# Seat scatter, lookup and edge-row gathers of a graph network, from loops with index copies to written-out DMAs

## The reference

```python
h = jnp.maximum(_layernorm(x, axis=-1), 0.0)
# layer 0, twice: norm = dinv[s] * dinv[d], with every node also its own neighbour
agg = jax.ops.segment_sum(norm[:, None] * h[s], d, num_segments=n); h = agg @ W.T + b
# layer 1
agg = jax.ops.segment_sum(jax.nn.relu(h[src] + edge_attr), dst, num_segments=n)
# layer 2, 8 steps: softmax of the edges of one destination, then
h = jax.ops.segment_sum(h[src] * a[:, None], dst, num_segments=n); th = th + h * temp[k + 1]
# layer 3, 10 steps: src_norm from the count of each source, dst_norm from that of each destination
h = jax.ops.segment_sum((h * src_norm[:, None])[src], dst, num_segments=n) * dst_norm[:, None]
out = out + w[step + 1] * h
```

## Time and profile before

| | |
|---|---|
| three timed runs | 8374.17, 8385.81, 8390.06 us; median 8385.81 |
| the profiled execution | 8379.78 us, its span 8378.1 us |
| POOL busy | 5656.5 us (68%), 5478 instructions |
| DVE busy | 5415.4 us (65%), 18625 instructions |
| PE busy | 1686.8 us (20%) |
| ACT busy | 822.6 us (10%) |
| chain that ended last, by engine | POOL 46%, issue 22%, DVE 20%, DMA 7% |
| of it, POOL gathers into `pair` | 5% |
| of it, POOL scatters into `seatmap` | 5% |

### The profile page before, as it was taken

One profiled execution on the slowest core, in us unless ns is written; L12 is line 12 of the kernel. 1 busy time (PEld: TensorE's weight loads), 2 busy tenths in 40 slices (PEclk: granted clock), 3 DMA queues, 4 the chain that ended last, 5 costly groups with the idle time before them and its releaser, 6 DMA issues.

```text
span 8378.1 us, 61926 instructions
## 1 busy us (share of the span) xinstructions
PE 1686.8 (20%) x7784; PEld 1230.3 (15%) x7784; DVE 5415.4 (65%) x18625; ACT 822.6 (10%) x2010; POOL 5656.5 (68%) x5478
## 2 busy tenths in 40 slices
PE   5744435310355135500022102000000000000000
PEld 1233324210244023400022101000000000000000
DVE  6778868758988634367788788666556664445520
ACT  0011112100122431100000000000006000000000
POOL 6777767656777767667677573666650767777767
PEclk8755555555555555555555555555555555555555
DMA  7034424310355433933444213243232222433310
GB/s 260 0 88 96 95 63 108 74 34 6 88 126 131 102 96 99 299 85 106 122 110 111 68 46 81 48 44 46 40 33 87 47 61 50 42 43 43 38 22 19
DMA packets 1198007, 661.31 MB, mean 79 GB/s; under 512 B 1057323, under 2 KB 1070560, under 8 KB 1195204
## 3 DMA queue, kind: packets, MB, share of 16 engines
q10 hardware_dynamic: 880608, 373.78, 16.4%
q0 software_dynamic: 174720, 155.54, 12.7%
q1 hardware_dynamic: 142436, 129.95, 5.2%
HBM read 236.69 MB, written 425.58 MB: 79 GB/s over the span
## 4 chain that ended last, share of the span: by engine, by line
POOL 46%; issue 22%; DVE 20%; DMA 7%; ACT 3%; DVEq 1%; POOLq 1%; ACTq 1%; SPq 0%; PE 0%
POOL G L575 20%; POOL X L575 12%; DVE G L2154 5%; POOL pair L575 5%; POOL seatmap L579 5%; POOL out L579 4%; ACT wide_block L1160 2%; POOL wide_block L575 1%; DVE xm L1648 1%; DVE st L1618 1%; DVE G L2466 1%; DMA raw<-G 1%; DMA G<-alt_d,idxC 1%; DMA G<-tab,idxA 1%; ACT rowsB L1160 1%
## 5 line engine op out<-in xcount | busy, mean ns | idle before, releaser
L575 POOL DMA_INDIRECT G<-tab,idxA x1008 | 1082.4, 1074 | 341.1 <-issue 322.1
L575 POOL DMA_INDIRECT X<-flagtab,X x588 | 624.1, 1061 | 231.4 <-issue 229.5
L575 POOL DMA_INDIRECT G<-alt_e,idxC x420 | 438.0, 1043 | 145.7 <-issue 133.1
L1309 PE MATMUL TR<-w4T,shared 128*128 128x64 f32 x2356 | 493.7, 405 | 156.3 <-ACT shared L1024 156.3
L575 POOL DMA_INDIRECT pair<-lookup,idxs x392 | 421.4, 1075 | 142.6 <-issue 118.4
L1309 PEld LDWEIGHTS TR<-w4T,shared 128*128 128x128 f32 x2356 | 480.2, 315 | 250.1 <-issue 250.1
L575 POOL DMA_INDIRECT X<-in_x,dst_gat x392 | 422.5, 1078 | 124.7 <-issue 124.7
L579 POOL DMA_INDIRECT seatmap<-vals,idxs x392 | 406.3, 1036 | 140.8 <-issue 116.7
L575 POOL DMA_INDIRECT G<-alt_d,idxC x392 | 402.4, 1026 | 138.7 <-issue 132.2
L1618 DVE BATCH_NORM_STATS2 st<-xin 128x6 f32<-128x64 f32 x3136 | 419.3, 211 | 112.4 <-issue 63.6
L1326 PE MATMUL HP<-ident,tcar 128*64 128x128 f32 (+1 forms) x21 | 8.7, 415 | 2268.3 <-DVEq L1543 2257.7
(11 more groups left out here) (523 smaller groups left out, 7698.7 us busy)
## 6 DMA issues: line engine op xcount, KB each, us to landing
tab<-wide_block ACTq DMA_DIRECT2D x294, 448.0 KB, 3.8
tab<-rowsB ACTq DMA_DIRECT2D x98, 448.0 KB, 2.7
xin<-tab SPq DMA_DIRECT2D x84, 448.0 KB
raw<-G ACTq DMA_DIRECT2D x84, 448.0 KB
xin<-in_x SPq DMA_DIRECT2D x56, 448.0 KB, 5.0
tab<-wide_block ACTq DMA_DIRECT2D x2, 12544.0 KB, 55.5
out<-shared ACTq DMA_DIRECT2D x56, 448.0 KB, 5.9
staged<-wide_block SPq DMA_DIRECT2D x20, 1120.0 KB, 5.6
```

What stands on the lines that cost most here:

```text
L575: pool.indirect_dma_start(to, None, table, bass.IndirectOffsetOnAxis(ap=index, axis=0), bounds_check=bound, oob_is_err=False).then_inc(s, 16)
L1309: last = nc.tensor.matmul(T[:, r * D:(r + 1) * D], U[:, r % 2, r // 2, :], w4T[:, :], start=True, stop=True)
```

## The change

The two buffers `vals` and `pair` are removed (112 and 224 bytes per partition), so everything that is allocated after them lies lower. The seat scatter becomes 392 scatters in a row that take their indices and values straight from `end0` and `place0`; the two semaphores are waited for once, behind the last. The lookup becomes 392 gathers in a row that read `src0` and write straight into `found`; again one wait for each semaphore, behind the last. The ten chunks of edge rows are written out, with indices straight from `eidx` and constant waits; the waits on `attr_stored` and `attr_gathered` stay. The ten POOL registers that counted these semaphores are gone.

```diff
-            def seat(c, s):
-                pool.tensor_copy(idxs[:, s, :], cols(end0, c))
-                pool.tensor_copy(vals[:, s, :], cols(place0, c)).then_inc(pool_step, 1)
-                pool.wait_ge(pool_step, r_step.more(1))
-                pool.sem_inc(pool_waited, 1)
-                last_row(seatmap)
-                for j in range(CH):
-                    scatter(seatmap, idxs[:, s, j:j + 1], vals[:, s, j:j + 1], seated[s])
-            def seat_landed(s):
-                pool.wait_ge(seated[s], r_seat[s].more(16 * CH))
-                pool.sem_inc(pool_waited, 1)
-            for s in (0, 1):
-                seat(s, s)
-            with pool.Fori(1, NCH // 2) as i:
-                for s in (0, 1):
-                    seat_landed(s)
-                    seat(2 * i + s, s)
-            for s in (0, 1):
-                seat_landed(s)
+            for c in range(NCH):
+                for j in range(c * CH, c * CH + CH):
+                    scatter(seatmap, end0[:, j:j + 1], place0[:, j:j + 1], seated[c % 2])
+            for s in (0, 1):
+                pool.wait_ge(seated[s], 16 * CH * (NCH // 2))
...
-            def find(c, s):
-                pool.tensor_copy(idxs[:, s, :], cols(src0, c)).then_inc(pool_step, 1)
...
-                    gather(pair[:, s, j, :], lookup, idxs[:, s, j:j + 1], found_some[s])
-            def keep(c, s):
-                pool.wait_ge(found_some[s], r_fs2[s].more(16 * CH))
-                pool.sem_inc(pool_waited, 1)
-                pool.tensor_copy(found[:, ds(c * CH, CH), :], pair[:, s, :, :]).then_inc(pool_step, 1)
...
+            for c in range(NCH):
+                for j in range(c * CH, c * CH + CH):
+                    gather(found[:, j, :], lookup, src0[:, j:j + 1], found_some[c % 2])
+            for s in (0, 1):
+                pool.wait_ge(found_some[s], 16 * CH * (NCH // 2))
             pool.sem_inc(found_all, 1)
...
-            def attr_rows(c, first):
-                pool.tensor_copy(idxs[:, 0, :], cols(eidx, c)).then_inc(pool_step, 1)
-                pool.wait_ge(pool_step, r_step.more(1))
-                pool.sem_inc(pool_waited, 1)
+            def attr_rows(c):
                 last_row(edge_attr)
                 for h in (0, 1):
-                    if not first:
-                        pool.wait_ge(attr_stored[h], r_as[h].more(16))
-                        pool.sem_inc(pool_waited, 1)
+                    if c:
+                        pool.wait_ge(attr_stored[h], 16 * c)
                     for j in range(h * half, h * half + half):
-                        gather(G[:, 1, j, 0:D], edge_attr, idxs[:, 0, j:j + 1], attr_gathered[h])
+                        gather(G[:, 1, j, 0:D], edge_attr, eidx[:, c * CH + j:c * CH + j + 1], attr_gathered[h])
...
-            with pool.Fori(1, HEAD) as c:
-                attr_rows(c, False)
+            for c in range(HEAD):
+                attr_rows(c)
...
-                    gather(edge_slot[s][:, j, :], edge_attr, idxs[:, s, j:j + 1], edges_gathered[s])
+                    gather(edge_slot[s][:, j, :], edge_attr, eidx[:, c * CH + j:c * CH + j + 1], edges_gathered[s])
```

More of the change, by code:

```diff
@@ L143, in _build @@
         look = sb("look", [P, 2, CH])
-        vals = sb("vals", [P, 2, CH])
-        pair = sb("pair", [P, 2, CH, 2])
         xin = sb("xin", [P, 2, CH, D])
@@ L559, in _ @@
             r_lk = [Reached(pool, f"pool_lk{s}") for s in (0, 1)]
-            r_seat = [Reached(pool, f"pool_seat{s}") for s in (0, 1)]
-            r_fs2 = [Reached(pool, f"pool_found{s}") for s in (0, 1)]
             r_fg = Reached(pool, "pool_fg")
@@ L639, in _ @@
             last_row(lookup)
-            def find(c, s):
-                pool.tensor_copy(idxs[:, s, :], cols(src0, c)).then_inc(pool_step, 1)
-                pool.wait_ge(pool_step, r_step.more(1))
-                pool.sem_inc(pool_waited, 1)
-                last_row(lookup)
-                for j in range(CH):
-                    gather(pair[:, s, j, :], lookup, idxs[:, s, j:j + 1], found_some[s])
-            def keep(c, s):
-                pool.wait_ge(found_some[s], r_fs2[s].more(16 * CH))
-                pool.sem_inc(pool_waited, 1)
-                pool.tensor_copy(found[:, ds(c * CH, CH), :], pair[:, s, :, :]).then_inc(pool_step, 1)
-                pool.wait_ge(pool_step, r_step.more(1))
-                pool.sem_inc(pool_waited, 1)
-            for s in (0, 1):
-                find(s, s)
-            with pool.Fori(1, NCH // 2) as i:
-                for s in (0, 1):
-                    keep(2 * i + (s - 2), s)
-                    find(2 * i + s, s)
-            for s in (0, 1):
-                keep(NCH - 2 + s, s)
+            for c in range(NCH):
+                for j in range(c * CH, c * CH + CH):
+                    gather(found[:, j, :], lookup, src0[:, j:j + 1], found_some[c % 2])
+            for s in (0, 1):
+                pool.wait_ge(found_some[s], 16 * CH * (NCH // 2))
             pool.sem_inc(found_all, 1)
@@ L740, in _ @@
             gather(X[:, FC, :], x, fidx[:, F_DST:F_DST + 1], x_front)
-            with pool.Fori(HEAD, MID) as c:
-                attr_rows(c, False)
+            for c in range(HEAD, MID):
+                attr_rows(c)
             for k in KINDS:
@@ L749, in _, with edge_rows @@
             pool.wait_ge(seats_cleared, 64)
-            r_es2 = [Reached(pool, f"pool_edges{s}") for s in (0, 1)]
-            def edge_rows(c, s, first=False):
-                if not first:
-                    pool.wait_ge(edges_stored[s], r_es2[s].more(16))
-                    pool.sem_inc(pool_waited, 1)
-                pool.tensor_copy(idxs[:, s, :], cols(eidx, c)).then_inc(pool_step, 1)
-                pool.wait_ge(pool_step, r_step.more(1))
-                pool.sem_inc(pool_waited, 1)
+            def edge_rows(c, s):
                 last_row(edge_attr)
                 for j in range(CH):
-                    gather(edge_slot[s][:, j, :], edge_attr, idxs[:, s, j:j + 1], edges_gathered[s])
-            edge_rows(MID, 0, True)
+                    gather(edge_slot[s][:, j, :], edge_attr, eidx[:, c * CH + j:c * CH + j + 1], edges_gathered[s])
+            edge_rows(MID, 0)
             for h in (0, 1):
                 pool.wait_ge(attr_stored[h], 16 * MID)
-            edge_rows(MID + 1, 1, True)
+            edge_rows(MID + 1, 1)
             for s in (0, 1):
```

12 lines of the change are left out of this document (3 added, 9 removed).

## The result

The changed kernel takes 8330.15 us (median of 4 runs, 8328.49 to 8332.57), the kernel before 8385.84 (4 runs, 8374.17 to 8390.06): ratio 0.9936, 95% interval 0.9919 to 0.9953. It is faster by 55.7 us, where 47.1 were forecast and 8338 us. The profiled execution took 8332.57 us with a span of 8330.9, almost to the digit what the sum gave from the profiled execution of before (8332.7 and 8331). That agreement is luck: three terms that the sum did not have, 3.3 and 7.5 us lost and 10.9 gained, cancel in this pair of profiles, and only the last of them belongs to the change.

The account below looks back on a forecast made before the run. DVE's 47.08 us wait for POOL's scatter and lookup was taken as the bound; POOL's 59 us saving is capped at 47.1. 8379.78 less 47.1 gives 8332.7; with the median 6.0 above the profile, 8338 us, range 8316 to 8364.

Parts of the forecast that it names:

- What bounds, and the cap: At found_all DVE waits for POOL's scatter and lookup; POOL saves 56 to 70 us, gain capped at 47.1 us.
- The boundary as the price: Between chunks the pause shrinks to 0.30 us: 0.93 us less per scatter chunk, 1.25 per lookup chunk, together 58.9 us.
- The five waits: DVE's five waits for look_done, 124.8 us together, stay as they are, only earlier.
- the edge rows: Ten written-out chunks save POOL up to 0.92 us each, 9.2 us in all; costed at nothing because covered.
- the moved buffers: Buffers behind vals and pair move: no change, 10 us either way; rival has slower stores lose some 20 us, 8358, chance 0.06.
- Stalls of the written-out code: Rival: POOL's written-out code meets a 7.32 us pause every 98 DMAs, eight cost 59 us; 8386, chance 0.05.
- Pile-up: Rival: 392 unheld scatters fill their queue and run at landing pace; found_all 187 us later, 8573 us, chance 0.03.
- all 47.1 us are carried to the end: Behind found_all (1161 us) no load, store or wait is tied to anything else, so the whole 47.1 us lasts.
- The base: The sum starts from one profiled execution of the kernel before: 8379.78 us, span 8378.1, with timed median 6.0 us above.

Follow-up runs that it names:

- the parts alone: Kernel before with one part each: seat scatter only 8350.85 us, lookup only 8343.30 us, edge rows only 8385.75 us; kernel before beside them 8388.98 us.
- the half that was moved: Changed kernel with DVE's dense pairs cut into halves and one half moved into the fourth look_done wait: 8312.22 us, ratio 0.9909.
- the old places: Changed kernel with the two removed buffers allocated again, unused, so later buffers lie where they lay before: 8327.00 us, ratio 0.9918.

## Why the prediction was right, and where it was not

- *What bounds, and the cap.* Right. POOL saved 60.2 us by the two stretches (23.4 + 36.8), within the 56 to 70 forecast; the scatter took 537 us (531 to 547), the lookup 553 (547 to 556), POOL's wait for the flags 23.4 (16 to 30), and DVE's wait went to 0.66. The cap at DVE's own arrival is shown by the parts alone, which do not add up, and by the half that was moved and found the unused 15 us. What POOL saved beyond that was idle, as the forecast had it.
- *The boundary as the price.* Right, and for the scatter now shown: 0.93 us a chunk goes with the copies and POOL's wait for them. The prediction had said that the wait for landed chunks does not end the pause; with the copies gone, keeping it or not makes no difference (8351.13 and 8350.85 us). For the lookup the size is near (33.8 us by the boundaries, 36.8 measured), and its parts were not separated.
- *The five waits, the edge rows, the moved buffers.* Right: 123.8 us, so nothing of the gain was given back there; no difference for the edge rows alone; no difference for the places. POOL's 35.59 us before `tab<-fown` lie above the 24 to 33 that the prediction gave as a sign; that wait varies by itself, from 24.06 to 30.5 us between two profiles of the kernel before. The edge rows saved POOL some 4 us, not up to 9: its lead is 43.8 us at the flags' store and 47.8 at the end of its last gather (2967.19 less 2919.35). The wait for `attr_stored` had taken part of the copy's place. The twenty staging stores land in 5.9 us against 5.6; over all profiles it is 5.0 to 5.9 with the old places and 5.5 to 5.9 with the new.
- *Stalls of the written-out code.* Void, as forecast, though the sign that the prediction named for them, pauses of several microseconds inside the 392, is there. The kernel before has as many, ahead of the same scatters. In the kernel before and then in the changed one:

```profile
202.57 0.99 POOL L579 DMA_INDIRECT seatmap<-vals,idxs  x1 [2.19 <-issue]
...
359.73 0.98 POOL L579 DMA_INDIRECT seatmap<-vals,idxs  x1 [2.19 <-issue]
```

```profile
198.00 0.99 POOL L575 DMA_INDIRECT seatmap<-X  x1 [5.04 <-issue]
...
348.67 0.98 POOL L575 DMA_INDIRECT seatmap<-X  x1 [1.69 <-issue]
```

  There are three over a microsecond in the scatter, in the lookup and in the x rows of every one of the fourteen profiles, always ahead of the 114th, the 226th and the 338th of the 392 transfers, in loops and in written-out code alike, and three of 2.19 us in the scatter that was written out with its copies. So they are no price of written-out code; what happens every 112 transfers, no run shows. The pauses of the scatter that reads in place are longer, 10.4 us together in the changed kernel against 6.6 before, so the 23.4 us that the scatter saved are net of 3.9 us lost there. The Trainium skill, "Runtime: NRT & Kernel Launch", section "Instruction fetch mechanics", has straight code streamed at almost no cost, and the trace agrees: written out with its copies the scatter costs no more than as a loop (ratio 0.9998). The same section of the Trainium skill has a taken branch stall where its target lies outside the two blocks that the engine holds; POOL's loop shows no such stall, since writing it out gained nothing, and whether its body reaches beyond two blocks no run here shows.
- *Pile-up.* Void. Without any wait the mean scatter is 1041 ns against 1036, and the kernels that read in place with and without the waits take the same time.
- *The step that failed: that all 47.1 us are carried to the end and nothing else happens.* The prediction saw nothing behind 1161 us that the change touches, and so costed the layers at nothing. They gave another 10.9 us in this pair of profiles, 13.1 in the mean of fourteen, and 12 by the medians when the old scatter was put back. That the medians differ by 55.7 us and not 47.1, and that the forecast of 8338 us is 8 us too high, is in the main this term; it is known by what it goes with, and its cause is open.
- *The base.* The sum was made against one execution in which the waits at the loop's exit came to 5.30 us; a second profile of the same kernel had 11.51. Such a place is worth finding before a difference of a few microseconds between two profiles is explained. Here it helped to make the profiled times agree to 0.2 us for the wrong reason.

## What to carry to other kernels

When a wait is to be taken away, look first at who would be late next: the gain ends there, and the rest of the saving lies idle on the other engine until work is moved across, which was worth another 44 us here. In a staged loop on POOL look at the pause at the chunk boundary and at what ends it; in the seat scatter here it was POOL's own copy, and indices read in place removed it, while the loop and the landing waits cost nothing. Check two profiles of the unchanged kernel against each other before a small term of a comparison is believed.

## What the runs showed of the hardware

A gather of 128 rows issued by POOL takes about 1.0 us and is followed by a 0.30 us pause, and this pace is a property of the program: 1309 and 1310 ns from start to start (median of the intervals behind the seat scatter and the lookup) in two runs of the kernel before, 1302 in both runs of the changed kernel. It followed the form of the seat scatter at the program's start through all fourteen profiles, 1309 to 1312 ns where the scatter reads from copies and 1302 to 1305 where it reads in place. The stores `out<-X,dst_out` take 982 to 984 ns in the mean where scatter and lookup both copy their indices, 978 to 981 where one of the two is in place, and 971 to 973 where both are, so these follow the lookup's form too. The cause is open.

Inside a run of 392 such transfers POOL pauses for 1.2 to 6 us ahead of the 114th, 226th and 338th, in scatters, lookups and x rows of all fourteen profiles; the cause of that is open too.
